# An attention block on one core: queries and keys split into f16 high and low parts under one power of two, and a reordered opening

## What is computed

```python
h = maximum(layernorm(x), 0)
q, k, v = split_heads(h @ Wq.T), split_heads(h @ Wk.T), split_heads(h @ Wv.T)   # 16 heads of 32
a = einsum('bhnd,bhmd->bhnm', q, k) * 512 ** -0.5 + (adj + adj)[:, None]
row_nonzero = any(a != 0, axis=-1, keepdims=True)
p = softmax(where(row_nonzero, a, -inf)); p = where(isnan(p), 0, p)
out = x + (einsum('bhnm,bhmd->bhnd', p, v) merged over heads) @ Wo.T
```

## Time and profile before

| | busy us | share of the span |
|---|---|---|
| PE | 1245.4 | 97% |
| PEld | 1109.5 | 86% |
| DVE | 1114.6 | 87% |
| ACT | 1054.7 | 82% |
| POOL | 884.3 | 69% |

### The profile page before, as it was taken

One profiled execution on the slowest core, in us unless ns is written; L12 is line 12 of the kernel. 1 busy time (PEld: TensorE's weight loads), 2 busy tenths in 40 slices (PEclk: granted clock), 3 DMA queues, 4 the chain that ended last, 5 costly groups with the idle time before them and its releaser, 6 DMA issues. The chain is left out here.

```text
span 1285.5 us, 43965 instructions
## 1 busy us (share of the span) xinstructions
PE 1245.4 (97%) x13104; PEld 1109.5 (86%) x13104; DVE 1114.6 (87%) x4006; ACT 1054.7 (82%) x2427; POOL 884.3 (69%) x1262
## 2 busy tenths in 40 slices
PE   4899999999999999999999999999999999999996
PEld 4788988888988888988888988888988888888885
DVE  6798889888889898889898889898889898888884
ACT  4788888888888888888888888888888888888885
POOL 1676677776677776777776777776777766777765
PEclk9999999999999999999999999999999999999999
DMA  6344554554544554554554544554544554544541
GB/s 228 84 108 119 143 122 118 143 131 116 145 122 116 145 130 114 147 122 115 147 129 114 149 121 114 148 127 114 151 119 114 150 125 115 152 118 114 135 116 57
DMA packets 90772, 163.88 MB, mean 127 GB/s; under 512 B 14976, under 2 KB 23168, under 8 KB 90752
## 3 DMA queue, kind: packets, MB, share of 16 engines
q1 hardware_dynamic: 90752, 163.64, 48.9%
HBM read 46.14 MB, written 16.78 MB: 49 GB/s over the span
## 5 line engine op out<-in xcount | busy, mean ns | idle before, releaser
L884 POOL TENSOR_TENSOR fold<-minus 128x512 f32<-128x512 f32 x256 | 327.4, 1279 | 293.6 <-DVE bounds L739 293.5
L567 ACT ACTIVATE probs<-minus,bounds 128x256 f32<-128x256 f32 x1024 | 459.5, 498 | 23.8 <-DVE bounds L739 23.8
L748 DVE TENSOR_TENSOR pT_lo<-pT_ps,pT_hi 128x512 f16<-128x512 f32 x512 | 351.3, 686 | 62.5 <-ACT pT_hi L578 59.3
L578 ACT ACTIVATE pT_hi<-pT_ps 128x512 f16<-128x512 f32 x512 | 304.9, 595 | 109.7 <-PE pT_ps L403 108.1
L739 DVE CUSTOM_DVE_ANT_0 minus<-s_ps,adj_now 128x256 f32<-128x256 f32 x1024 | 388.5, 416 | 5.9 <-ACT probs L567 4.7
L403 PE MATMUL pT_ps<-ident,probs 128*128 128x128 f32 x2048 | 307.6, 273 | 1.8 <-ACT probs L567 1.6
L328 PE MATMUL job_ps<-hT_hi,w_hi 128*128 128x256 f16 x1024 | 280.2, 274 | 1.4 <-DVE w_lo L689 0.9
L328 PE MATMUL job_ps<-hT_hi,w_lo 128*128 128x256 f16 x1024 | 279.0, 272 | 0.0
L328 PE MATMUL job_ps<-hT_lo,w_hi 128*128 128x256 f16 x1024 | 278.8, 272 | 0.0
L403 PEld LDWEIGHTS pT_ps<-ident,probs 128*128 128x128 f32 x2048 | 241.8, 140 | 19.4 <-ACT probs L567 3.0
L392 PE MATMUL s_ps<-qk_stack 96*128 96x256 f32 x1024 | 246.4, 323 | 0.7 <-DVE w_lo L689 0.7
(11 more groups left out here) (77 smaller groups left out, 2253.0 us busy)
## 6 DMA issues: line engine op xcount, KB each, us to landing
qk_stack<-qk_parts SPq DMA_DIRECT2D x768, 128.0 KB, 2.3
x_in<-x SPq DMA_DIRECT2D x32, 512.0 KB, 3.4
x_res<-x SPq DMA_DIRECT2D x32, 512.0 KB, 3.7
out<-y SPq DMA_DIRECT2D x64, 256.0 KB, 2.1
adj_in<-adj SPq DMA_DIRECT2D x32, 256.0 KB, 3.5
w_in<-wq SPq DMA_DIRECT2D x2, 512.0 KB, 6.7
w_in<-wk SPq DMA_DIRECT2D x2, 512.0 KB, 8.2
w_in<-wv SPq DMA_DIRECT2D x2, 512.0 KB, 7.9
```

What stands on the lines that cost most here:

```text
L567: end = nc.scalar.activation(probs[hh % 2][:, t, :], minus[hh // 2 % 2][:, hh % 2, t, :], ACT.Exp, bias=bounds[:, hh // 2 % 4, 2 * (hh % 2 ...
L578: nc.scalar.activation(pT_hi[hh % 4][:, :, :], pT_ps[hh % 2][:, :].rearrange("p (m n) -> p m n", m=NT), ACT.Copy).then_inc(pT_high, 1)
L748: nc.vector.tensor_tensor(pT_lo[hh % 4][:, :, :], pT_ps[hh % 2][:, :].rearrange("p (m n) -> p m n", m=NT), pT_hi[hh % 4][:, :, :], ALU.sub ...
L884: nc.gpsimd.tensor_tensor(f1[:, :, :], src[:, :, 0:N // 2], src[:, :, N // 2:N], ALU.add).then_inc(folded1, 1)
```

## The change

- Queries and keys, `qk_parts` and `qk_stack`, are f16 instead of fp32r, so that the score matmuls (L392) have f16 operands. f16 has a small range: one power of two `z` for all scores is found on the chip from the greatest product of Q's and K's scales. `top_scale` takes the greatest per partition, PE transposes it across partitions, `score_scales` makes `z`, `1/z`, `-2z` and the scale of Q. `copy_adj` multiplies the adjacency by `1/z`, and `shift` multiplies by `-2z` instead of -2.
- The opening takes Q's and K's second halves third and fourth. Three of the six extents are sums of magnitudes made by ACT (`sum_weight`) instead of maxima made by DVE. Five of the six halves are scaled on POOL instead of ACT. The first head's scores, bound and exponentials come earlier, between the projections. The output weight's high and low parts move into the first batch (ACT at heads 3 and 5, POOL at heads 5 and 7).

```diff
-W_TOP, H_TOP = 2.0 ** 14, 2.0 ** 9
+W_TOP, SUM_TOP, H_TOP = 2.0 ** 14, 2.0 ** 15, 2.0 ** 9
...
-    UNTOP = 1.0 / (W_TOP * H_TOP)
+    QK_UNTOP = 2.0 ** -18
+    V_UNTOP = 1.0 / (2.0 * SUM_TOP)
     HALF_SCALE = 0.5 * float(D) ** -0.5
+    Z_OF_TOP = 2.0 ** 13
+    Q_UNTOP = HALF_SCALE / (H_TOP ** 2 * QK_UNTOP)
...
-        TURNS = [(WQ, 0), (WK, 0), (WV, 0), (WV, 1), (WQ, 1), (WK, 1)]
+        TURNS = [(WQ, 0), (WK, 0), (WQ, 1), (WK, 1), (WV, 0), (WV, 1)]
+        SUMMED = [(WQ, 1), (WV, 0), (WV, 1)]
...
-        qk_parts = sb("qk_parts", [P, 2, 4, 2, N], F32R)
-
-
-        qk_stack = sb("qk_stack", [3 * HD, 2, G, 2, 2, N], F32R)
+        qk_parts = sb("qk_parts", [P, 2, 4, 2, N], F16)
+
+
+        qk_stack = sb("qk_stack", [3 * HD, 2, G, 2, 2, N], F16)
...
-                pe.wait_ge(w_scaled, at + 1)
+                if at == 0:
+                    pe.wait_ge(first_scaled, 1)
+                else:
+                    pe.wait_ge(w_scaled, at)
...
+            turn(WQ, 0)
             for n in range(2):
                 job("h", n, 0, 0, 4, 0)
-            turn(WQ, 0)
             turn(WK, 0)
+            turn(WQ, 1)
             weight_waits(pe, WQ, 0)
+
+            pe.wait_ge(top_steps, 2)
+            nc.tensor.transpose(pT_ps[0][:, 0:P], top[:, 0:1].to_broadcast([P, P]), ident[:, :]).then_inc(top_turned, 1)
             job("qk", 0, 0, 0, 12, 0)
             weight_waits(pe, WK, 0)
             job("qk", 0, 0, 12, 24, 0)
             job("qk", 1, 0, 0, 24, 0)
+            pe.wait_ge(top_steps, 3)
+            turn(WK, 1)
             turn(WV, 0)
             turn(WV, 1)
-            turn(WQ, 1)
-            turn(WK, 1)
             weight_waits(pe, WV, 0)
             job("v", 0, 0, 0, 12, 0)
-            weight_waits(pe, WK, 1)
-            for hh in range(AHEAD):
-                scores(0, hh, True)
+            scores(0, 0, True)
             job("qk", 2, 0, 0, 24, 0)
+            scores(0, 1, True)
             job("v", 1, 0, 0, 12, 0)
+            weight_waits(pe, WV, 1)
+            scores(0, 2, True)
...
-            def scale_weight(i, half):
-
-                act.wait_ge(w_scales, TURNS.index((i, half)) + 1)
-                for k in range(2 * half, 2 * half + 2):
-                    end = nc.scalar.activation(w_in[i][:, k, :], w_in[i][:, k, :], ACT.Copy,
-                                               scale=w_scale[:, i, UNSCALE, k:k + 1])
-                end.then_inc(w_scaled, 1)
+            def scale_first_weight():
+
+                act.wait_ge(w_scales, 1)
+                for k in range(2):
+                    end = nc.scalar.activation(w_in[WQ][:, k, :], w_in[WQ][:, k, :], ACT.Copy,
+                                               scale=w_scale[:, WQ, UNSCALE, k:k + 1])
+                end.then_inc(first_scaled, 1)
+
+            def sum_weight(i, half):
+
+
+                spare = [y[:, k, :] for k in range(2)] if i == WQ else [
+                    minus[half][:, k, :, :].rearrange("p t n -> p (t n)") for k in range(2)]
+                act.wait_ge(w_loaded[i][half], 16)
+                for k in range(2):
+                    at = 2 * half + k
+                    end = nc.scalar.activation(spare[k], w_in[i][:, at, :], ACT.Abs,
+                                               accum_out=w_scale[:, i, EXTENT, at:at + 1])
+                end.then_inc(w_sum, 1)
...
-                nc.scalar.activation(adj_now[:, :, :], adj_in[:, :, :], ACT.Copy).then_inc(adj_copied, 1)
-
-            scale_weight(WQ, 0)
-            scale_weight(WK, 0)
+                nc.scalar.activation(adj_now[:, :, :], adj_in[:, :, :], ACT.Copy,
+                                     scale=one_by_z[:, 0:1]).then_inc(adj_copied, 1)
+
+            scale_first_weight()
+            sum_weight(WQ, 1)
+            high_weight(WQ, 0)
             for n in range(2):
                 take("h", n, 0)
-            high_weight(WQ, 0)
             high_weight(WK, 0)
-            scale_weight(WV, 0)
-            scale_weight(WV, 1)
+            high_weight(WQ, 1)
+            sum_weight(WV, 0)
             act.wait_ge(q_scales, 1)
-            for n in range(2):
-                take("qk", n, 0, True)
+            take("qk", 0, 0, True)
+            sum_weight(WV, 1)
+            take("qk", 1, 0, True)
+            high_weight(WK, 1)
             high_weight(WV, 0)
             high_weight(WV, 1)
-            scale_weight(WQ, 1)
-            scale_weight(WK, 1)
             copy_adj(0)
-            high_weight(WQ, 1)
-            high_weight(WK, 1)
             take("v", 0, 0, True)
-            high_out_weight(0)
-            act.wait_ge(q_scales, 2)
+            exponentials(0, 0, True)
...
+                    if first and hh in (3, 5):
+
+                        high_out_weight(hh // 2 - 1)
...
+            def top_scale():
+
+
+                nc.vector.scalar_tensor_tensor(qk_scale[:, :], w_scale[:, WQ, SCALE, :], 1.0, w_scale[:, WK, SCALE, :],
+                                               ALU.mult, ALU.mult).then_inc(top_steps, 1)
+                dve.wait_ge(top_steps, 1)
+                nc.vector.tensor_reduce(top[:, :], qk_scale[:, :], AX_X, ALU.max).then_inc(top_steps, 1)
+
+            def score_scales():
+
+
+                dve.wait_ge(top_turned, 1)
+                nc.vector.tensor_reduce(z[:, :], pT_ps[0][:, 0:P], AX_X, ALU.max).then_inc(top_steps, 1)
+                dve.wait_ge(top_steps, 3)
+                nc.vector.tensor_scalar(z[:, :], z[:, :], LEAST_SCALE, Z_OF_TOP, ALU.max, ALU.mult
+                                        ).then_inc(top_steps, 1)
+                dve.wait_ge(top_steps, 4)
+                nc.vector.reciprocal(one_by_z[:, :], z[:, :]).then_inc(top_steps, 1)
+                nc.vector.tensor_scalar(minus_two_z[:, :], z[:, :], -2.0, None, ALU.mult).then_inc(top_steps, 1)
+                dve.wait_ge(top_steps, 6)
+                nc.vector.tensor_scalar(q_scale[:, :], qk_scale[:, :], one_by_z[:, 0:1], Q_UNTOP, ALU.mult, ALU.mult
+                                        ).then_inc(q_scales, 1)
+                dve.wait_ge(q_scales, 1)
...
-                        in1=adj_now[:, t, :], scale=-2.0, scalar=GREATEST, op0=ALU.add, op1=ALU.min,
+                        in1=adj_now[:, t, :], scale=minus_two_z[:, 0:1], scalar=GREATEST, op0=ALU.add, op1=ALU.min,
...
+            weight_extent(WQ, 0)
             weight_scales(WQ, 0)
+            weight_extent(WK, 0)
             weight_scales(WK, 0)
+            weight_extent(WK, 1)
+            weight_scales(WQ, 1)
+            weight_scales(WK, 1)
+            dve.wait_ge(w_scales, 4)
+            top_scale()
+            low_weight(WQ, 0)
             for n in range(2):
                 take("h", n, 0)
-            low_weight(WQ, 0)
             low_weight(WK, 0)
-            dve.wait_ge(w_scales, 2)
-            query_scales(0)
+            score_scales()
+            low_weight(WQ, 1)
+            take("qk", 0, 0)
             weight_scales(WV, 0)
             weight_scales(WV, 1)
-            for n in range(2):
-                take("qk", n, 0)
+            take("qk", 1, 0)
+            low_weight(WK, 1)
             low_weight(WV, 0)
             low_weight(WV, 1)
-            weight_scales(WQ, 1)
-            weight_scales(WK, 1)
-            dve.wait_ge(w_scales, 6)
-            query_scales(1)
-            low_weight(WQ, 1)
-            low_weight(WK, 1)
             take("v", 0, 0)
+            shift(0, 0, True)
             take("qk", 2, 0)
-            for hh in range(2):
-                shift(0, hh, True)
+            shift(0, 1, True)
...
+            def scale_weight(i, half):
+
+                pool.wait_ge(w_scales, TURNS.index((i, half)) + 1)
+                for k in range(2 * half, 2 * half + 2):
+                    end = nc.gpsimd.tensor_scalar(w_in[i][:, k, :], w_in[i][:, k, :],
+                                                  w_scale[:, i, UNSCALE, k:k + 1], None, ALU.mult)
+                end.then_inc(w_scaled, 1)
...
+            normalise(0, True)
+            for i, half in TURNS[1:]:
+                scale_weight(i, half)
             for half in range(2):
-                low_out_weight(half)
-
-            pool.wait_ge(wo_split, 2)
+                scale_out_weight(half)
             fold(0, 0, True)
...
+                    if first and hh in (5, 7):
+                        low_out_weight((hh - 5) // 2)
```

More of the change, by code:

```diff
@@ L153, in attention_block @@
         EXTENT, SCALE, UNSCALE = range(3)
+        qk_scale = sb("qk_scale", [P, KT])
         q_scale = sb("q_scale", [P, KT])
-        wo_in = [o, sb("wo_in1", [P, 2, D])]
+        top = sb("top", [P, 1])
+        z, one_by_z, minus_two_z = sb("z", [P, 1]), sb("one_by_z", [P, 1]), sb("minus_two_z", [P, 1])
+        wo_in = [sb(f"wo_in{half}", [P, 2, D]) for half in range(2)]
         stats = sb("stats", [P, NT, 6])
@@ L249, in stack @@
                     for r, pair in enumerate((slice(1, 3), slice(0, 3, 2), slice(1, 4, 2))):
```

(36 more changed lines are left out.)

23 lines of the change are left out of this document (8 added, 15 removed).

## The result

The five runs of the changed kernel have a median of 1293.13 us (1291.90 to 1296.27) against 1286.66 us for the five of the kernel before: a ratio of 1.0051, with an interval of 1.0039 to 1.0063. The change makes the kernel 6.5 us slower, where the forecast had 1286.0 with a range of its own of 1280 to 1292. The profiled execution of after is the fastest of the five: 1291.9 us, with a span of 1290.1 against 1285.5. The traces can therefore explain 4.6 us; 1.9 us of the difference between the medians lies outside them.

A forecast was written before the change was run, and what follows sets the result against it. DVE was taken to bound heads 0 to 4 of each batch and PE heads 5 to 15. 1287.3 + 7 (shift charge less f16 gain) - 8 (opening) gave 1286.3, or 1286.0 us against the median; range 1280 to 1292.

The follow-up runs named there:

- b_open1: Kernel after with fp32r parts, constant in the shift, adjacency unscaled, no power of two, POOL's scaling still one operation; 1286.74 us, ratio 0.9995.
- a_const: Kernel after with the constant -2.0 in the shift instead of the per-partition value, leaving z out of the logits; 1275.55 us, ratio 0.9905.
- a_pool2: Kernel after with POOL's scaling of the weight halves written as two operations (second times 1.0) instead of one; 1287.92 us, ratio 1.0006.
- b_open2: Kernel after with fp32r parts, constant in the shift, adjacency unscaled, no power of two, POOL's scaling as two operations; 1280.89 us, ratio 0.9952.
- a_late: a_pool2 with layer-norm statistics moved to heads 8 and 13, aggregation to 14, and the output weight's pieces placed as in c_out; 1255.96 us, ratio 0.9753.
- c_out: b_open2 with first-batch output weight's high halves as four pieces at heads 6, 7, 9, 11, POOL's low halves at 9, 13; 1280.30 us, ratio 0.9943.
- b_mom2: Kernel before with the layer norm's moments moved from DVE's stretch to heads 8, 12 and 13 of the batch ahead; 1265.55 us, ratio 0.9823.

## What to carry to other kernels

A price is that of a form, not of an operation: before taking a duration from the nearest row, compare its number of operations, its pointer operands and its engine, and where one differs, put both ends into the sum. An average busy share of 87% can hide a stretch in which an engine sets the pace: find where it waits for nobody, and count what an edit adds or takes there. Here 1.5 us of unrelated work moved out of such a stretch was worth more (22 us) than the f16 scores (11 us), and it only paid once its data had landed by the new place. One trace of each kernel does not settle a difference of a microsecond in the opening, where landings and the clock move by more.

## What was not expected of the hardware

- POOL's `tensor_scalar` on 128x512 f32 takes 1.54 us with one operation and 0.68 us with two, at the same place; seen in after, b_open1 and a_const against a_pool2, b_open2 and the others. Why was not tried.
- While POOL ran the one-operation form, small DVE instructions were stretched. Rows of after, then of a_pool2, from the same steps on 128x2 and 128x4 values:

```profile
12.46 0.57 DVE L698 TENSOR_SCALAR w_scale<-w_scale 128x2 f32<-128x2 f32 x1
13.06 0.62 DVE L702 TENSOR_SCALAR w_scale<-w_scale 128x2 int32<-128x2 int32 x1
...
18.52 0.66 DVE L728 TENSOR_SCALAR q_scale<-qk_scale,one_by_z 128x4 f32<-128x4 f32 x1
```

```profile
13.37 0.15 DVE L698 TENSOR_SCALAR w_scale<-w_scale 128x2 f32<-128x2 f32 x1
13.55 0.19 DVE L702 TENSOR_SCALAR w_scale<-w_scale 128x2 int32<-128x2 int32 x1
...
18.69 0.23 DVE L728 TENSOR_SCALAR q_scale<-qk_scale,one_by_z 128x4 f32<-128x4 f32 x1
```

b_open1 and a_const show the first two again (0.57 and 0.63 in each); L711 at 13.91, a SCALAR_TENSOR_TENSOR between them, kept its 0.16. The Trainium skill (SBUF — State Buffer, Who interferes with whom) has it that a `tensor_scalar` on VectorE can need a port pair that it shares with GpSimd, and that the loser is blocked for the whole of the other's instruction. Two of the three long ones agree: they end at 13.02 and 19.18, POOL's second L957 of six at 13.00 and its sixth at 19.16. So does one beside a two-operation instruction of POOL, in a_late: 0.42 us, to 9.18, where POOL's `h` ends at 9.15. The one from 13.06 to 13.68 ends at no such point, but 0.68 us behind one, and so does a shorter one (0.38 us, from 11.75 to 12.13; POOL's first ends at 11.45). b_open1 and a_const have both again, at the same 0.68. That is the length of a two-operation instruction, so POOL may let go of the port once within the one-operation form; no run tests it, and the `tensor_scalar` instructions of 128x1 at 18.09 and 18.36 were not stretched at all.
- A per-partition scale in place of a constant costs 61 ns on the custom DVE operation of 128x256 (477 against 416; the shortest of 1024 with it takes 467, the longest without it 426), and 93 ns on ACT's copy of the adjacency (726 against 633).
- At the end of the program what follows the last transposes of probabilities takes 16.0 us at full granted clock (after, c_out, b_mom2) and 17.4 to 18.5 where the clock from the last body on is 0.92 to 0.95 (the other kernels).
